# Attention kernel on one core: queries and keys through a 128-lane stage and twelve transfers per unit, with a reordered schedule around it

## What is computed

```python
x1 = x + attn(cond(x))                    # x: (8, 256, 1024), float32
x  = x1 + ffn(cond2(x1))
# cond:  x @ W.T + b, plus (x @ A[slot]) @ B[slot] * 2, rank 16, one slot per batch
# attn:  32 query heads, 8 key and value heads of 32 channels, softmax, then @ w_o
# cond2: x1 @ weight[slot].T, one 1024 x 1024 matrix per batch
# ffn:   4 experts of rank 16; logits = h @ router.T, the best 2 of 4 by softmax
```

## Time and profile before

| | |
|---|---|
| median of 3 runs | 1136.36 us (1133.98 to 1136.42) |
| the profiled execution | 1136.62 us |
| its span (first to last instruction) | 1134.6 us |
| PE busy | 1040.4 us, 92% |
| DVE, ACT, POOL busy | 736.8, 419.6, 219.6 us |
| fold, to the first unit of attention | 0 to 162.7 us |
| attention to step 12 of the last pair | to 743.4 us |
| attention running out, batch 0 of the last stage | to 838.5 us |
| batches 1 to 7, 40.3 us each | to 1118 us |

### The profile page before, as it was taken

How to read it: one execution, slowest core, us unless ns; L and a number is a source line. 1 busy time by engine, 2 the same in 40 slices (tenths; PEclk the granted TensorE clock), 3 DMA queues, 4 the chain that set the end, 5 groups by cost and what they waited for, 6 DMA issues and landing times.

```text
span 1134.6 us, 17247 instructions
## 1 busy us (share of the span) xinstructions
PE 1040.4 (92%) x6934; PEld 832.4 (73%) x6934; DVE 736.8 (65%) x1237; ACT 419.6 (37%) x718; POOL 219.6 (19%) x160
## 2 busy tenths in 40 slices
PE   7999998998799988899987999969689999999995
PEld 6877787875468766678755787648479889898885
DVE  6562634587886788776886867884465566466553
ACT  5112132344453445443534535642342222313320
POOL 1000020232122222222221224651211100111100
PEclk9999998998899999899987999979899999999997
DMA  6022121011411113211123113343346455546530
GB/s 243 22 73 73 64 75 28 21 43 36 118 39 30 39 34 99 55 34 40 34 62 87 48 44 108 94 130 152 124 155 219 151 179 204 184 139 217 168 111 38
DMA packets 43231, 108.22 MB, mean 95 GB/s; under 512 B 6018, under 2 KB 23554, under 8 KB 39056
## 3 DMA queue, kind: packets, MB, share of 16 engines
q1 hardware_dynamic: 33424, 72.52, 20.5%
q0 software_dynamic: 9728, 34.61, 9.9%
HBM read 77.73 MB, written 18.36 MB: 85 GB/s over the span
## 4 chain that ended last, share of the span: by engine, by line
PE 77%; DVE 9%; ACT 6%; POOL 3%; DMA 2%; issue 2%; SPq 0%; POOLq 0%; DVEq 0%; ACTq 0%
PE psP L720 16%; PE psW L976 15%; PE psF L238 11%; PE psG L1175 7%; PE psS L762 4%; PE psP L735 4%; PE psT L773 4%; PE psO L786 4%; POOL p_sum L502 3%; PE psO L790 3%; PE psX L1196 3%; ACT probs L552 2%; DVE q_stack L602 2%; ACT q_stack L518 2%; PE psY L1215 2%
## 5 line engine op out<-in xcount | busy, mean ns | idle before, releaser
L720 PE MATMUL psP<-x_hl,wq 128*128 128x512 f32 x960 | 249.2, 408 | 10.4 <-DVE q_stack L602 10.4
L622 DVE TENSOR_REDUCE nmax<-psS 128x2 f32<-128x512 f32 x256 | 164.6, 684 | 124.2 <-PE psS L762 122.5
L502 POOL TENSOR_TENSOR p_sum<-probs 128x1024 f32<-128x1024 f32 x64 | 153.1, 2392 | 461.6 <-ACT probs L552 461.6
L720 PEld LDWEIGHTS psP<-x_hl,wq 128*128 128x128 f32 x960 | 183.4, 198 | 45.2 <-issue 10.9
L976 PE MATMUL psW<-wq 128*128 128x256 f32 x1536 | 198.7, 285 | 6.7 <-issue 4.5
L976 PEld LDWEIGHTS psW<-wq 128*128 128x128 f32 x1536 | 192.1, 192 | 12.3 <-issue 4.7
L552 ACT ACTIVATE probs<-psT 128x512 f32<-128x512 f32 x256 | 139.0, 595 | 100.6 <-PE psT L773 99.9
L1063 DVE TENSOR_TENSOR cond_lo<-cond_raw,cond_hi 128x1024 fp32r<-128x1024 f32 x64 | 77.6, 1223 | 79.2 <-ACT cond_hi L1018 79.2
L1018 ACT ACTIVATE cond_hi<-cond_raw 128x1024 fp32r<-128x1024 f32 x64 | 66.8, 1056 | 153.0 <-PE psG L1175 153.0
L635 DVE RECIPROCAL rden<-psO 128x256 f32<-128x256 f32 x64 | 112.0, 1750 | 13.2 <-PE psO L790 13.2
L762 PEld LDWEIGHTS psS<-k_stack,q_stack 96*128 96x128 f32 x512 | 84.0, 200 | 30.6 <-DVE nmax L622 18.1
(11 more groups left out here) (113 smaller groups left out, 1227.7 us busy)
## 6 DMA issues: line engine op xcount, KB each, us to landing
cond_raw<-in_cond POOLq DMA_DIRECT2D x64, 512.0 KB, 4.6
x_raw<-in_xT SPq DMA_DIRECT2D x32, 256.0 KB, 4.6
q_stack<-q_stack SPq DMA_DIRECT2D x32, 256.0 KB, 3.1
o_scratch<-o_sb SPq DMA_DIRECT2D x64, 128.0 KB, 2.1
o_raw<-o_scratch SPq DMA_DIRECT2D x8, 1024.0 KB, 5.1
x_sb<-in_xT SPq DMA_DIRECT2D x8, 1024.0 KB, 7.4
outT<-x_sb SPq DMA_DIRECT2D x8, 1024.0 KB, 6.5
q_raw<-in_Wqkv SPq DMA_DIRECT2D x24, 256.0 KB, 4.3
```

What stands on the lines that cost most here:

```text
L502: pool.tensor_tensor(p_sum[:], probs[:, 0], probs[:, 1], ALU.add).then_inc(sum_done, 1)
L622: dve.tensor_reduce(nmax[:, n % 2, 2 * hp:2 * hp + 2, qt], psS[:, i % 2].rearrange("p (h k) -> p h k", h=2), AX.X, ALU.max, negate=True).t ...
L720: mm = pe.matmul(out, wq[:, i, w, k * P:(k + 1) * P], x[:, k, part], start=(k == 0 and n_ == 0), stop=False)
```

## The change

- **Stage.** ACT copies a whole unit, 128 partitions by 512, into `stage_hi`, DVE subtracts into `stage_lo`. SyncE (`send`) then issues twelve DMAs of 32 partitions, 64 KB each: four heads to the high rows, four to their second copy, four to the low rows. The stage is one buffer: a unit's ACT copy waits until the twelve of the unit before have landed (`wait_stage`). What waited for q_stack's slot on ACT now waits on SyncE, and a transfer into a slot that is still read is issued up to two steps later (`sent`). PE waits for the landings alone.
- **Order of the units.** WORK spreads the slices more evenly over the steps. q1 of pair 0 moves behind the first scores. x of the next pair is loaded and split one step earlier, three of its tiles on POOL.
- **Small things.** POOL adds the probabilities in two halves. The transposition of the maxima also waits until ACT has emptied psM. The first row tile of the fold runs its high x high products before the low parts are there.
- **Last stage.** w_o and o are loaded earlier, and batch 0's tiles run at steps 12 to 15. Rows 0 to 5 of batch 0 run at steps 16 to 18, ahead of each half's other work; rows 4 to 7 are still loaded by POOL after its last sum. A row's low part is written over its raw data, so that its buffer is free when PE has read it. The gates' ranks come from one comparison of all pairs of experts, on wider operands: 11 waits between DVE operations instead of 16. Each batch is stored in four parts.

```diff
+        def first_row_tile():
+            for i, (w, q) in enumerate(((w_hi, q_hi), (w_hi, q_lo), (w_lo, q_hi))):
+                if i == 0:
+                    pe.wait_ge(w_hi_done, 1)
+                    pe.wait_ge(q_hi_done, 1)
+                elif i == 1:
+                    pe.wait_ge(q_lo_done, 1)
+                else:
+                    pe.wait_ge(w_lo_done, 1)
+                for m in range(KT):
+                    pe.matmul(psF[:, bank(0, m)], w[:, 0, m * P:(m + 1) * P], q[:, 0], start=(i == 0), stop=False)
...
-    (["k1:4-8"], ["q4:0-2"]),
-    (["q4:2-5"], ["q4:5-8"]),
-    (["q5:0-4"], ["q5:4-5"]),
-    (["q5:5-8"], ["q6:0-2"]),
-    (["q6:2-4"], ["q6:4-6"]),
-    (["q6:6-8"], ["q7:0-3"]),
+    (["k1:4-8"], ["q4:0-3"]),
+    (["q4:3-6"], ["q4:6-8", "q5:0-1"]),
+    (["q5:1-4"], ["q5:4-6"]),
+    (["q5:6-8", "q6:0-1"], ["q6:1-4"]),
+    (["q6:4-8"], ["q7:0-3"]),
     (["q7:3-6"], ["q7:6-8"]),
     ([], ["+u"]),
-    (["+k0:0-4"], ["+k0:4-8"]),
-    (["+q0:0-4"], ["+q0:4-8"]),
-    (["+q1:0-4"], ["+q1:4-8"]),
+    (["+k0:0-3"], ["+k0:3-6"]),
+    (["+k0:6-8", "+q0:0-2"], ["+q0:2-5"]),
+    (["+q0:5-8", "+q1:0-1"], ["+q1:1-4"]),
+    (["+q1:4-6"], ["+q1:6-8"]),
 ]
+FIRST = {0: (["q1"], ["v0"]), 1: (["q2:0-4"], ["q2:4-8"])}
...
+def query_slot(p, g):
+    return (G * p + g) % QS
+def slot_read(p, g):
+    return 2 * (G * p + g - QS) + 1
+def sent(n, part):
+    units = []
+    for m in range(max(n - 2, 0), n + 1):
+        for q in range(2):
+            for p, u in finished(m, q):
+                if u[0] in "qk":
+                    w = slot_read(p, int(u[1:])) + 2 if u[0] == "q" else 0
+                    if (n, part) == max((m, q), (w, 1)) if w > 0 else (n, part) == (m, q):
+                        units.append((p, u))
+    return units
...
+    stage_hi, stage_lo = at("stage_hi", [P, T2], F32R, R1 + 4096), at("stage_lo", [P, T2], F32R, R1 + 6144)
...
+    def wait_landed(eng, p, u):
+        j = int(u[1:])
+        if u[0] == "q":
+            eng.wait_ge(q_landed[query_slot(p, j)], 16 * COPIES * ((G * p + j) // QS + 1))
+        else:
+            eng.wait_ge(k_landed[j], 16 * COPIES * (p + 1))
+    def wait_stage(eng, p, u):
+        i = SEQ_QK.index(u)
+        if p or i:
+            wait_landed(eng, p if i else p - 1, SEQ_QK[i - 1])
...
-        def double(p, u):
-            j = int(u[1:] or 0)
-            if u[0] in "qk":
-                sp.wait_ge(proj_act, unit(p, u) + 1)
+        def send(p, u):
+            j = int(u[1:])
             if u[0] == "q":
-                slot = (G * p + j) % QS
-                sp.dma_start(f(q_stack[64:96, slot]), f(q_stack[0:32, slot])).then_inc(q_dup[slot], 16)
-            elif u[0] == "k":
-                sp.dma_start(f(k_stack[32:64, :, 4 * j:4 * j + 4]),
-                             f(k_stack[0:32, :, 4 * j:4 * j + 4])).then_inc(k_dup[j], 16)
+                slot = query_slot(p, j)
+                if slot_read(p, j) >= 0:
+                    sp.wait_ge(st_done, TILES * (slot_read(p, j) + 1))
+                rows, landed = (0, 64, 32), q_landed[slot]
+            else:
+                if p:
+                    sp.wait_ge(st_done, TILES * (STEPS * (p - 1) + 8 * (j + 1)))
+                rows, landed = (0, 32, 64), k_landed[j]
+            for i, row in enumerate(rows):
+                if i == 0:
+                    sp.wait_ge(proj_act, unit(p, u) + 1)
+                if i == 2:
+                    sp.wait_ge(proj_dve, dve_unit(p, u) + 1)
+                for h in range(HG):
+                    to = q_stack[row:row + 32, slot, :, h] if u[0] == "q" else k_stack[row:row + 32, :, 4 * j + h]
+                    stage = stage_lo if i == 2 else stage_hi
+                    sp.dma_start(f(to), f(both(stage[32 * h:32 * h + 32]))).then_inc(landed, 16)
...
-            for unit_ in evacuated(n, 0):
-                double(*unit_)
+            for unit_ in sent(n, 0):
+                send(*unit_)
             if n >= 3:
                 po, go, co, _ = where(n - 3)
                 sp.wait_ge(o_copied, n - 2)
                 sp.dma_start(oT[2 * po + co, :, go], o_sb[:, (n - 3) % 2]).then_inc(o_stored[(n - 3) % 2], 16)
             if more:
-                for k in {10: range(0, 3), 11: range(3, KT)}.get(s, ()):
+                for k in {9: range(0, 3), 10: range(3, KT)}.get(s, ()):
                     load_x(sp, p + 1, k)
-            for unit_ in evacuated(n, 1):
-                double(*unit_)
-            if more and s == 12:
+            for unit_ in sent(n, 1):
+                send(*unit_)
+            if more and s == 11:
...
-        for u in ("k0", "q0", "q1"):
-            double(0, u)
+        for u in ("k0", "q0"):
+            send(0, u)
...
-            pool.wait_ge(exp_done, TILES * (n + 1))
-            if n:
-                pool.wait_ge(pv_done, n)
-            pool.tensor_tensor(p_sum[:], probs[:, 0], probs[:, 1], ALU.add).then_inc(sum_done, 1)
+            for hp in range(2):
+                pool.wait_ge(exp_done, TILES * n + 2 * hp + 2)
+                if n and hp == 0:
+                    pool.wait_ge(pv_done, n)
+                heads = slice(hp * T2, (hp + 1) * T2)
+                pool.tensor_tensor(p_sum[:, heads], probs[:, 0, heads], probs[:, 1, heads], ALU.add).then_inc(sum_done, 1)
+            if (n + 2) % STEPS == 10 and p + 1 < PAIRS:
+                for k in range(XP):
+                    split_x_lo(pool, p + 1, k)
...
+        def copy_stage(p, u):
             act.wait_ge(proj_done, unit(p, u) + 1)
-            for h in range(HG):
-                ins = nc.scalar.activation(to(h), both(psP[32 * h:32 * h + 32, bank(p, u)]), ACT.Copy)
-                if h == 1:
-                    ins.then_inc(half_hi, 1)
-            ins.then_inc(proj_act, 1)
-        def copy_k(p, j):
-            if p:
-                act.wait_ge(st_done, TILES * (STEPS * (p - 1) + 8 * (j + 1)))
-            copy_heads(p, f"k{j}", lambda i: k_stack[0:32, :, 4 * j + i])
-        def copy_q(p, g):
-            slot, read_by = (G * p + g) % QS, 2 * (G * p + g - QS) + 1
-            if read_by >= 0:
-                act.wait_ge(st_done, TILES * (read_by + 1))
-            copy_heads(p, f"q{g}", lambda h: q_stack[0:32, slot, :, h])
+            wait_stage(act, p, u)
+            nc.scalar.activation(stage_hi[:], psP[:, bank(p, u)], ACT.Copy).then_inc(proj_act, 1)
...
-                for k in range(3, KT):
+            if more and s == 11:
+                for k in range(XP, KT):
...
+            elif u[0] in "qk":
+                dve.wait_ge(proj_act, unit(p, u) + 1)
+                dve.tensor_tensor(stage_lo[:], psP[:, bank(p, u)], f(stage_hi[:]), ALU.subtract).then_inc(proj_dve, 1)
...
+            if n:
+                pe.wait_ge(rows_done, n)
...
+    ROWS_SPLIT = {15: [0, 1], 16: [2, 3], 17: [4, 5], 18: [6]}
+    ROWS_MULT = {(16 + k // 2, k % 2): k for k in range(6)}
+    WO_LOAD = {2: [0], 3: [1, 2], 4: [3, 4], 5: [5], 6: [6], 7: [7]}
     WO_FREE = ["q1", "q1", "q1", "q2", "v3", "v3", "q3", "k1"]
-    WO_SPLIT = {4 + k: k for k in range(KT)}
-    FIRST_TILES = {(14 + m // 2, m % 2): m for m in range(KT)}
+    WO_SPLIT = {3 + k: k for k in range(KT)}
+    FIRST_TILES = {(12 + m // 2, m % 2): m for m in range(KT)}
...
+    cond_raw, cond_lo = at("cond_raw", [P, RAW, D], F32, R1 + 4096), at("cond_lo", [P, RAW, D], F32R, R1 + 4096)
+    cond_hi = at("cond_hi", [P, SPLIT, D], F32R, R0 + 24576)
...
-        if s == 12:
-            sp.wait_ge(before.proj_done, PAIRS * NS)
+        if s == 8:
+            sp.wait_ge(before.proj_done, unit(PAIRS - 1, "q5") + 1)
             for i in range(2):
                 sp.wait_ge(before.o_stored[i], 16 * G)
             load_o(sp, 0)
+        if s == 11:
+            sp.wait_ge(before.proj_done, PAIRS * NS)
             load_x(sp, 0)
+            sp.dma_start(ra_raw[:], RA).then_inc(const_landed, 16)
...
-            sp.wait_ge(y_added, YT * (n + 1))
-            sp.dma_start(outT[n], x_sb[:, n % 2]).then_inc(stored, 16)
+            for j in range(YT):
+                sp.wait_ge(y_added, YT * n + j + 1)
+                sp.dma_start(outT[n, :, 2 * j:2 * j + 2], x_sb[:, n % 2, 2 * j:2 * j + 2]).then_inc(stored, 16)
...
-                pool.wait_ge(cond_lo_done, KT * n + k - RAW + 1)
+                pool.wait_ge(cond_used, KT * n + k - RAW + 1)
...
+        for r in ROWS_SPLIT.get(s, ()):
+            cond_row_hi(act, r)
...
+        if part == 1:
+            for r in ROWS_SPLIT.get(s, ()):
+                cond_row_lo(dve, r)
...
-            pool.wait_ge(before.proj_done, PAIRS * NS)
+            before.wait_landed(pool, PAIRS - 1, "q7")
...
+        k = ROWS_MULT.get((n - LAST, part))
+        if k is not None:
+            cond_row(pe, 0, k)
...
-            for k in range(KT):
-                cond_row(0, k)
+            for k in (6, 7):
+                cond_row(pe, 0, k)
```

229 lines of the change are left out of this document (109 added, 120 removed).

## The result

The changed kernel takes **1195.35 us** (median of 4 runs, 1191.74 to 1202.21) where the kernel before took 1136.01: ratio 1.0545, 95% interval 1.0511 to 1.0579. The forecast was 1103, with 1085 to 1126 as its range. The profiled execution spans 1196.0 us, 61.4 more than before.

A forecast was written before the change was run, and what follows sets the result against it. The prediction took PE's idle time, and the slow clock after it, as the bound. Its terms: 1136.6 - 1.3 + 8.7 - 24 - 2.5 - 11 - 3.2 = 1103 us, range 1085 to 1126.

The forecast's parts named there:

- Term 2: Stage transfers: twelve DMAs a unit on SyncE's queue at 0.60 us each, 7.2 us a unit, last landing 1.8 later.
- a step of 9.2 us hides that: Attention steps: a 9.2 us step covers the 7.2 us a unit holds SyncE's queue and the landing 1.8 later.
- The forecast's own sign of being wrong: In attention: PE waiting for q_landed inside steps would show the forecast wrong; no size given.
- The text's own slope: Whole kernel: each 0.1 us on the issue price moves the forecast time by some 10 us.
- The 1088 us: Whole kernel: with dispatch near 50 ns, issues cost 0.6 us a unit and the sum ends near 1088.
- SyncE becomes the bound: Rival, attention pairs: gains used up from about 0.93 us per issue; at 1.05, 12 us slower, 1149; chance 0.09.
- Term 3: Start of attention: q0 waits for k0's landing, scores at 191.4 instead of 188.39, q1 still to do; loss 8.7.
- The gain of 1.3 from the first row tile: Program start: first matmul no longer waits for the low part, 6.17 instead of 7.48 us.
- Term 4: Attention pairs: stall falls from 24.0 to about 16 us; gain 8 per pair, 24 over three boundaries, 2.5 last pair.
- Two small terms: Within each pair's remaining stall: 1.5 us for late nmax rows in step 8, 1.0 for k0's low-rank operands.
- Term 5: Attention running out into the last stage: 84.2 us instead of 95.2, gain 11; 3 if row 4 landed at 13.2.
- Term 6: End: shorter gate operations gain 1.8, smaller last store 1.4; gain 3.2 us in all.

The follow-up runs named there:

- run 3: Changed kernel without the second copy of the high parts after each place's first use, eight transfers a unit instead of twelve: 1138.06 us, ratio 1.0052.
- run 6: Changed kernel with the four transfers of the second copy issued by ScalarE, the other eight by SyncE: 1132.62 us, ratio 1.0006 to the kernel before.
- e_actdup_olddrain: Changed kernel with ScalarE issuing the second copy and the last stage as before, but new gates and stores: 1127.06 us.
- Run 8: Two kernels: changed kernel with the old last stage but new gates and stores, 1183.13 us; run 6 with batch 0's eight rows after attention, 1124.0 us.
- run 1: Kernel before with all of the change except staged copies, their transfers and the new order of units: 1145.61 us, ratio 1.0106.
- run 10: Five candidates: changed kernel with ScalarE issuing the second copy, varying last stage, order of units or x loads: 1115.78 to 1127.06 us.
- run 9: Kernel before with only the new end, gates in eleven dependent steps and the store in four parts: 1128.12 us, ratio 0.995.
- run 4: Changed kernel with the transfers through DRAM, four writes and three reads a unit instead of twelve transfers: 1219.37 us, ratio 1.077.

## Why the forecast was wrong

**Term 2, transfers, and the sentence "a step of 9.2 us hides that".** The price was right: 0.60 us forecast, 0.597 and a pitch of 0.64 measured; 7.7 us a unit for 7.2; landing 2.0 for 1.8. What failed is the comparison. I set the time that a unit holds the queue against the time of a step, a rate against a rate, and against the mean step. But steps 5 and 6, in which k1 and q4 are finished, take 8.5 and 7.9 us, while twelve sends with one step's maxima and store take 7.7 + 1.4 + 0.4 = 9.5: there the queue is full. Three units (q3, k1, q4) are projected in a row ahead of one deadline, the scores of step 8, and each goes its whole way through that queue, 9.9 to 10.9 us from copy to copy. The forecast's own sign of being wrong, PE waiting for q_landed inside steps, is what the trace shows. Runs 3 and 6 show the size: 2.5 us off each unit's sends are worth 57 and 63 us. The text's own slope (10 us for each 0.1 us of price, that is for 1.2 us a unit) would have given 21. The 1088 us that the forecast gives for issues of 50 ns does not follow from that slope either, by which 0.37 us already ends at 1080 to 1086. The rival *SyncE becomes the bound* was the right one, and its break-even of 0.93 us an issue was computed from occupancy (120 issues + 33 us), so it stood far from 0.64 and got 0.09. At 0.64 the same formula has the queue busy some 110 of the 163.6 us of a pair, two thirds, and it bound the kernel all the same.

The Trainium skill (DMA: Bandwidth & Descriptors, Rules for kernel authors) warns against many small transfers and says that under 64 KB one pays mostly overhead; these have just 64 KB. The forecast set it aside because they overlap in flight. They do: their landing stays at 2.0 us. The warning holds here for another reason, that issues do not overlap on one queue. The fixed 2.0 us and the 50 ns of dispatch that the forecast quotes stand in that page of the Trainium skill under the path of DMAs issued by GpSimd, while these are SyncE's: the landing of 2.0 us comes out the same, the issue takes 597 ns. The same page of the Trainium skill (Issuing engines are not separate DMA queues) says that issuing from several engines saves only the time to initiate a DMA, usually small beside the DMA itself. Here it is 0.60 us beside a landing of 2.0, 2.5 us a unit, and run 6 shows 63 us.

**Term 3, start.** Forecast a loss of 8.7; step 2 begins 8.8 us later (210.54 against 201.79). The total is right, in part by luck, because the forecast misread where it started from. It took 188.39 for the first scores of step 0 in the kernel before, but these are the second half of them:

```profile
183.57 0.71 PE L762 MATMUL psS<-k_stack,q_stack 96*128 96x256 f32 x4
188.39 1.39 PE L762 MATMUL psS<-k_stack,q_stack 96*128 96x256 f32 x4 [4.11 <-DVE nmax L622]
```

The changed kernel's first scores are at 192.45, so 8.9 us are lost ahead of them. From there to step 2 both need 18 us: q1's projection fills the time in which PE had waited 4.11 us for DVE and run at the lower level. The gain of 1.3 from the first row tile did not come: its first matmul is 0.74 us earlier, and by 162.6 us both kernels are level.

**Term 4, pairs.** Forecast 145 each, measured 162 to 164. With eight issues on SyncE the pairs take 145 to 150 (runs 3 and 6), so the rest of the change gained some 5 of the 8 us forecast a pair, and the queue took them and 10 us more. The longest step is the one I named, step 11 (16.6 us forecast, 20.8 measured in pair 1, 18.8 to 20.3 in e_actdup_olddrain). But x is only a part of it: PE's waits there are 3.1 us for the maxima's rows, 2.4 for the exponentials and 2.0 in three for x, and u runs at the lower level. Two small terms were badly wrong: 1.5 for the delays in step 8 (steps 7 to 9 take 31.2 us where before had 27.3), and 1.0 for k0's low-rank operands, which cost 12.4 us of waiting in the three pairs, up to 4.5 at once, and slow clock after it.

**Term 5, running out.** Forecast 84.2 from step 12 to the second batch, measured 103.1 (799.75 to 902.87, the second batch's first row), where before takes 95.0. Row 4's wait is as computed, 8.6 for 9.6. Not counted were the 5.30 us for which the third output tile waits for the residual's x (0.5 forecast), what two waits of 3.37 have beyond the 2.6 forecast, another 2.0, and the lower level after the longer ones: the second half of the stretch runs at a mean clock of 0.77. The wait for x is the queue again, since its load stands behind q7's twelve:

```profile
803.10 5.16 SPq L513 DMA_DIRECT2D q_stack<-stage_hi  x8
808.30 2.52 SPq L513 DMA_DIRECT2D q_stack<-stage_lo  x4
810.86 0.58 SPq L946 DMA_DIRECT2D x_sb<-in_xT  x1
...
816.62 4.80 PE L1028 MATMUL psW<-wq 128*128 128x256 f32 x24 [5.30 <-DVE x_sb L1014]
```

Run 8 shows that the rows moved to steps 16 to 18 cost more than they give. That the last pair, with the loads and roundings of w_o brought forward, would take 5 to 11 us more (runs 1, 8 and 10) was in no term.

**Term 6, end.** 3.2 forecast, 4.2 in the trace, 5.3 by run 9. Right: the wait for the gated rows is 3.40 instead of 5.80, and the stores land in 2.5 us (median) instead of 6.5.

## What to carry to other kernels

Before work moves from engines to a DMA queue, write the queue's order out with durations and follow one unit through it: from when its data exist, to when its last transfer has landed, to who needs it first. The issue time of small transfers counts serially in that, and so does all that stands between them in the queue; compare it with the shortest steps, not with the mean one. If the queue is what ends it, try a second issuing engine at a point where little stands behind it: here it was worth 63 us of 1195. Other issues, put ahead of the exponentials, cost more than they gave. And rows moved ahead of their data into a stretch where PE had nothing else to do were paid twice here, in the wait and in the clock after it.

## What the runs showed of the hardware

A transfer of 64 KB within SBUF takes the issuing sequencer 0.60 us, SyncE's (median 597 ns) and ScalarE's (619) alike, and lands 2.0 us after its issue even with twelve in a row. Two queues issuing at once did not lengthen the landing (medians 2.0 to 2.1 us in run 6). Writes to DRAM from the stage took 0.53 to 0.56 us to issue and reads back 0.32 (medians, run 4), and writes and reads together landed after 3.0 to 6.0 us, median 3.9.
